# Sandwich layer (clustered attention, then a mixture of experts), one core: routing per group of tokens, rows sent to regions, three held chunks instead of two

## What is computed

```python
x = x + ln(attn(ln(x)))         # attn: qk = x@Wqk, v = x@Wv; per batch and head (16 heads of 16 channels)
                                #   softmax over channel-by-channel distances of qk, times v, then @ Wo
h = layernorm(x, g, b)          # rows of 256
logits = h @ Wr                 # 7 routed experts; top 2, gates = softmax of the two logits
pos = place of each (token, choice) in its expert's queue, first choices of ALL tokens before second ones
keep = pos < 732                # capacity of each expert
routed = sum over kept choices of gate * (silu(xe@W1[e]) * (xe@W3[e])) @ W2[e]
shared = (silu(h@W1s) * (h@W3s)) @ W2s      # every token, hidden width 1024
x = x + ln(routed + shared)
```

## Time and profile before

| | us |
|---|---|
| median of 3 runs | 1268.76 (1264.95 to 1269.63) |
| the profiled execution, own time | 1270.08 |
| its span, first to last instruction | 1268.3 |
| PE busy | 1128.9 (89%) |
| DVE busy | 724.9 (57%) |
| POOL busy | 391.4 (31%) |
| mean granted TensorE clock | 0.941 of full |

### The profile page before, as it was taken

How to read it: one execution, slowest core, us unless ns; L and a number is a source line. 1 busy time by engine, 2 the same in 40 slices (tenths; PEclk the granted TensorE clock), 3 DMA queues, 4 the chain that set the end, 5 groups by cost and what they waited for, 6 DMA issues and landing times.

```text
span 1268.3 us, 20395 instructions
## 1 busy us (share of the span) xinstructions
PE 1128.9 (89%) x6932; PEld 1033.2 (81%) x6932; DVE 724.9 (57%) x1541; ACT 519.3 (41%) x916; POOL 391.4 (31%) x321
## 2 busy tenths in 40 slices
PE   3557999999999999999998698999999999999760
PEld 2456888988888888888887597999999999998650
DVE  4445684464764564845667994445354454454885
ACT  2313343434434344343444212545455455453543
POOL 4523120131210230300312485144343434213554
PEclk9566999999999999999998898999999999999985
DMA  4206212044110044110353103244253242255773
GB/s 141 83 17 226 74 51 67 13 145 177 52 52 30 34 151 151 67 51 17 103 180 100 34 1 111 81 119 113 47 129 91 73 124 54 42 163 163 237 260 130
DMA packets 84004, 125.38 MB, mean 99 GB/s; under 512 B 8645, under 2 KB 68553, under 8 KB 83921
## 3 DMA queue, kind: packets, MB, share of 16 engines
q1 hardware_dynamic: 73728, 113.80, 27.0%
q0 software_dynamic: 10192, 10.52, 4.9%
HBM read 76.30 MB, written 47.98 MB: 98 GB/s over the span
## 4 chain that ended last, share of the span: by engine, by line
PE 72%; DVE 9%; issue 8%; POOL 6%; ACT 3%; DMA 2%; SPq 1%; POOLq 0%; ACTq 0%; DVEq 0%
PE bank L975 21%; PE bank L976 21%; PE bank L977 21%; PE bank L997 2%; PE bank L1077 2%; POOL sb_t_scale L772 2%; DVE sb_st L1206 1%; PE bank L1179 1%; PE bank L1069 1%; DVE sb_x L1477 1%; POOL sb_x L436 1%; ACT sb_ln_o L817 1%; PE bank L987 1%; DVE sb_act L1358 1%; PE bank L1015 1%
## 5 line engine op out<-in xcount | busy, mean ns | idle before, releaser
L1358 DVE TENSOR_TENSOR sb_act<-bank,sb_act 128x512 f32<-128x512 f32 (+2 forms) x240 | 148.7, 620 | 406.5 <-PE bank L977 365.8
L975 PE MATMUL bank<-sb_h_hi,sb_wup_lo 128*128 128x512 f32 (+2 forms) x960 | 354.8, 370 | 18.1 <-DVE sb_h_lo L1345 9.1
L976 PE MATMUL bank<-sb_h_lo,sb_wup_hi 128*128 128x512 f32 (+2 forms) x960 | 351.0, 366 | 0.0
L977 PE MATMUL bank<-sb_h_hi,sb_wup_hi 128*128 128x512 f32 (+2 forms) x960 | 349.6, 364 | 0.0
L899 ACT ACTIVATE sb_act<-bank 128x512 f32<-128x512 f32 (+2 forms) x240 | 130.1, 542 | 477.0 <-PE bank L977 434.2
L975 PE MATMUL bank<-sb_wdn_hi,sb_act_lo 128*128 128x256 f32 (+1 forms) x848 | 252.6, 298 | 24.4 <-DVE sb_act_lo L1351 22.4
L977 PE MATMUL bank<-sb_wdn_hi,sb_act_hi 128*128 128x256 f32 (+1 forms) x848 | 241.2, 284 | 0.0
L976 PE MATMUL bank<-sb_wdn_lo,sb_act_hi 128*128 128x256 f32 (+1 forms) x848 | 241.0, 284 | 0.0
L975 PEld LDWEIGHTS bank<-sb_h_hi,sb_wup_lo 128*128 128x128 f32 x960 | 183.9, 192 | 36.6 <-issue 11.9
L977 PEld LDWEIGHTS bank<-sb_h_hi,sb_wup_hi 128*128 128x128 f32 x960 | 182.9, 191 | 22.0
L976 PEld LDWEIGHTS bank<-sb_h_lo,sb_wup_hi 128*128 128x128 f32 x960 | 183.9, 192 | 16.3
(11 more groups left out here) (195 smaller groups left out, 1452.5 us busy)
## 6 DMA issues: line engine op xcount, KB each, us to landing
sb_xin<-in_L_ffn_W_dram SPq DMA_DIRECT2D x28, 512.0 KB
sb_xin<-in_L_attn_x_dram SPq DMA_DIRECT2D x16, 512.0 KB, 3.6
sb_x<-in_L_attn_x_dram SPq DMA_DIRECT2D x16, 512.0 KB, 5.1
x_scratch<-sb_x SPq DMA_DIRECT2D x16, 512.0 KB, 5.7
u_scratch<-sb_u SPq DMA_DIRECT2D x16, 512.0 KB, 3.2
hT_scratch<-sb_hr SPq DMA_DIRECT2D x16, 512.0 KB, 2.8
sb_hfull<-hT_scratch SPq DMA_DIRECT2D x16, 512.0 KB, 3.9
y_scratch<-sb_ysb SPq DMA_DIRECT2D x14, 512.0 KB, 2.8
```

Source lines behind the costliest of these rows:

```text
L975: t_.matmul(o, a_lo, b_hi, start=start, stop=False, skip_group_check=True)
L976: t_.matmul(o, a_hi, b_lo, start=False, stop=False, skip_group_check=True)
L977: return t_.matmul(o, a_hi, b_hi, start=False, stop=stop, skip_group_check=True)
L1358: v.tensor_tensor(act[:, m % 2, 0:c.w], bank[(4 if c.wide and m % 2 else 0) + 1][:, 0:c.w], act[:, m % 2, 0:c.w], ALU.mult).then_inc(act_o ...
```

## The change

What it does:

- `u_route` on DVE now finds both choices of the group's 4 tiles (13 small instructions where 1 was). New steps `u_count` (PE: 11 small bf16 matmuls) and `u_slot` (DVE: 9 small instructions) 2 places later give every token the row it is sent to: region = (choice, expert), 768 rows each, or a spare row.
- POOL sends the rows: per group `u_send0..3`, in all 8 indirect writes of 128 rows of 258 values (256 of `u`, the token's number, the difference of its two logits), at timetable places 57, 61, 84 and 88 (+0..3). The first send of a group waits until the one before has landed. 128 such writes in all. `u` has four buffers; its plain store is gone.
- The routing over all tokens (stage 3 above) is gone; what is left is `indices`: 5 small DVE instructions, at place 9 of the only chunk there.
- `HELD` = 3: one shared chunk in stage 3, three in stage 5. `IN_HELD` = 15, spread over 40 places (`LAST_AT`). The third held chunk's `hfull` is loaded behind the first y loads.
- In stage 3 the low halves of expert 0's weights are DVE's (6 pieces), not POOL's.
- In stage 1 SP clears the regions: 15 transfers, 11776 rows of 1032 bytes, at places 14 to 27. SP waits for all constants first.
- PE turns both halves of `u`, and for b > 0 of `xn`, through bank 7 only, with a wait on the copy of the first half. POOL computes e^(difference) per expert chunk, DVE the gates (4 small instructions) and the scatter indices (1 copy).

Cut to its core:

```diff
-    HELD = 2
+    HELD = 3
+    UW = D + 2
+    SENT = 2 * GT * 16
+    ROOM = ST * P
-        IN_HELD = (2 * FM * HELD - LAST0) // 2
+        IN_HELD = min((2 * FM * HELD - LAST0) // 2, NG - 1)
+        LAST_AT = [LAST0 + g * (2 * FM * HELD - LAST0) // IN_HELD for g in range(IN_HELD)]
+        TIMES = 2 * PLACES - LEAD
         for q in range(GB):
             for name, at in (("o_mix", 0), ("o_stats", 1), ("o_norm", 3), ("o_add", 4), ("u_stats", 6),
-                             ("u_norm", 9), ("u_turn0", 10), ("u_turn1", 11), ("u_route", 12)):
+                             ("u_norm", 9), ("u_turn0", 10), ("u_turn1", 11), ("u_route", 12), ("u_count", 14),
+                             ("u_slot", 14)):
                 timetable[38 + 4 * q + at].append((name, q))
+        for q, at in enumerate((57, 61, 84, 88)):
+            for t in range(GT):
+                timetable[at + t].append((f"u_send{t}", q))
...
+                if place in CLEAR_AT:
+                    sp.dma_start(sent_t[CLEAR_AT.index(place)], zrow[:, :].rearrange("p (a w) -> p a w", a=1
+                                 ).broadcast_to([P, ST, UW])).then_inc(none_in, 16)
...
+            def u_send(t):
+                def step(b, q):
+                    if t == 0:
+                        pool.wait_ge(r_slot, OPEN + b * GB + (q + 1))
+                        if isinstance(b, int) and b == 0 and q == 0:
+                            pool.wait_ge(none_in, (2 * E + 1) * 16)
+                        elif q > 0:
+                            pool.wait_ge(sent[q - 1], b * SENT + SENT)
+                        else:
+                            pool.wait_ge(sent[GB - 1], b * SENT)
+                        pool.sem_inc(pool_go, 1)
+                    for c in range(2):
+                        pool.indirect_dma_start(sent_d, bass.IndirectOffsetOnAxis(ap=sendto[:, q, t, c:c + 1], axis=0),
+                                                u[q][:, t, :], None).then_inc(sent[q], 16)
+                return step
...
-            for place in range(PLACES - LEAD, PLACES):
+            for place in range(PLACES - LEAD, TIMES):
                 attend(steps, place, B - 1)
-            for j in range(PIECES):
-                low_piece(1, j, 1, stage_later)
-            pool.wait_ge(r_slots, 1)
-            for n in range(NBLK):
...
                 def step(b, q):
                     if k == 0:
                         pe.wait_ge(u_ok, OPEN + b * GB + (q + 1))
-                        pe.wait_ge(lg_ok, OPEN + b * GB + q)
+                        pe.wait_ge(xtlo_ok, OPEN + b * (2 * GB) + 2 * GB)
+                    pe.wait_ge(hT_ok, OPEN + b * (2 * GB) + (2 * q + k))
                     for t in range(GT):
-                        ins = t_.transpose(bank[6 + k][:, t * P:(t + 1) * P], u[:, t, k * P:(k + 1) * P], ident[:, :])
+                        ins = t_.transpose(bank[7][:, t * P:(t + 1) * P], u[q][:, t, k * P:(k + 1) * P], ident[:, :])
...
+            def u_count(b, q):
+                pe.wait_ge(r_oh, b * GB + (q + 1))
+                t_.matmul(counts, earlier[:, :], oh[:, :, :, :].rearrange("p t c e -> p (t c e)"),
+                          start=True, stop=False, skip_group_check=True)
+                of = [oh[:, t, :, :].rearrange("p c e -> p (c e)") for t in range(GT)]
+                for t in range(1, GT):
+                    for s in range(t):
+                        t_.matmul(counts[:, t * 2 * E:(t + 1) * 2 * E], onesb[:, :], of[s],
+                                  start=False, stop=False, skip_group_check=True)
+                for t in range(GT):
+                    ins = t_.matmul(totals, onesb[:, :], of[t], start=False, stop=(t == GT - 1),
+                                    skip_group_check=True)
+                ins.then_inc(r_cnt, 1)
...
             def u_route(b, q):
...
+                for c in range(2):
+                    ch.link(v.tensor_reduce(best[:, c, :], lg[:, :, :], AX.X, ALU.max))
+                    ch.link(v.tensor_tensor(same[:, :, :], lg[:, :, :], over_e(best[:, c, :]), ALU.is_equal))
+                    ch.link(v.tensor_tensor(same[:, :, :], same[:, :, :], of_e, ALU.mult))
+                    ch.link(v.tensor_reduce(first[:, :], same[:, :, :], AX.X, ALU.max))
+                    ins = v.tensor_tensor(oh[:, :, c, :], same[:, :, :], over_e(first[:, :]), ALU.is_equal)
...
+            def u_slot(b, q):
+                dve.wait_ge(r_cnt, g + 1)
...
+                ch.step(v.tensor_copy(sendto[:, q, :, :], pos[:, :, :]))
+                ch.settle()
+                dve.sem_inc(r_slot, 1)
...
             def last_pass(place):
-                if place >= LAST0:
-                    g = (place - LAST0) // 2
-                    if place % 2 == 0:
-                        last_stats(g)
-                    else:
-                        if g > 0:
-                            last_add(v, dve, g - 1, DVE_TILES, t_ok)
-                        last_bias(g)
+                if place in LAST_AT:
+                    last_stats(LAST_AT.index(place))
+                elif place - 1 in LAST_AT:
+                    g = LAST_AT.index(place - 1)
+                    if g > 0:
+                        last_add(v, dve, g - 1, DVE_TILES, t_ok)
+                    last_bias(g)
```

More of the change, by code:

```diff
@@ L350, in held_chunks, with stored @@
         def held_chunks(body, between=lambda place: None):
-            body(expert_chunk(E - 1, 1, 1), held_chunk(0), held_chunk(1), between)
-            body(held_chunk(0), held_chunk(1), None, lambda place: between(2 * FM + place))
+            seq = [expert_chunk(E - 1, 1, 1)] + [held_chunk(h) for h in range(HELD)] + [None]
+            for h in range(HELD):
+                body(seq[h], seq[h + 1], seq[h + 2], lambda place: between(2 * FM * h + place))
+        def stored(s):
+            return sum((n + HELD) % 2 == s for n in range(FIRST))
         NCH = NG + 2 * E
@@ L565, in _ @@
                 sp.sem_inc(sp_go, 1)
-            for j in range(PIECES):
+            for j in range(3):
+                load_piece(1, j, [W1[0], W3[0]], W2[0], stage_later)
+            if HELD < GB - 1:
+                load_h(b, 1)
+            for place in range(PLACES - LEAD, TIMES):
+                attend(steps, place, b)
+            for j in range(3, PIECES):
                 load_piece(1, j, [W1[0], W3[0]], W2[0], stage_later)
@@ L597, in _ @@
                 sp.dma_start(last_y[k], last_view(y_d[0:T, :], k)).then_inc(t_y[k], 16)
+            for h in range(2, HELD):
+                load_held(h)
             for g in range(NG):
@@ L1195, in _ @@
             for m in (FM - 2, FM - 1):
-                down(held_chunk(1), m)
+                down(held_chunk(HELD - 1), m)
         @block.vector
@@ L1337, in _, with low_piece @@
                      "m_softmax": m_softmax, "m_low": m_low, "o_stats": o_stats, "o_norm": o_norm,
-                     "u_stats": u_stats, "u_norm": u_norm, "u_route": u_route}
-            def prep(c):
+                     "u_stats": u_stats, "u_norm": u_norm, "u_route": u_route,
+                     "u_slot": u_slot}
+            def low_piece(w, j, wset, stage):
+                hi, lo, src = piece(j, wset, stage)
+                dve.wait_ge(w_hi, w * PIECES + (j + 1))
+                v.tensor_tensor(lo, src, hi.bitcast(F32), ALU.subtract).then_inc(w_lo, 1)
+            def prep(c):
+                if c.expert is not None:
+                    par = 1 - c.wset
+                    dve.wait_ge(gathered[c.slot], c.landed)
+                    if not (isinstance(c.expert, int) and c.expert < 2):
+                        dve.wait_ge(added[c.slot], c.expert * (16 * HALF) - 16 * HALF)
+                    v.tensor_copy(scur[:, par, c.slot, :], rows[:, c.slot, 0:HALF, TOK]).then_inc(e_dst, 1)
                 dve.wait_ge(hhi_ok, c.n + 1)
@@ new lines, in route @@
+            def route(place):
+                if place % 2 and 5 <= place < 5 + 2 * PIECES:
+                    j = (place - 5) // 2
+                    if j == 4:
+                        dve.wait_ge(sent[0], B * SENT)
+                    low_piece(1, j, 1, stage_later)
+                if place == INDEX_AT:
+                    indices()
+            cs = [None] + last_chunks() + [None]
+            for j in range(1, len(cs) - 1):
+                body(cs[j - 1], cs[j], cs[j + 1], lambda place: beside_last(steps, route, 2 * FM * (j - 1) + place))
```

507 lines of the change are left out of this document (232 added, 275 removed).

## The result

The changed kernel takes 1346.56 us (median of 4 runs, 1344.79 to 1346.73) against 1267.53 before; the ratio is 1.0621, 95% interval 1.0597 to 1.0645. The forecast was 1261, with a range of 1240 to 1296: wrong in sign and in size. The profiled execution took 1346.66, 76.6 us more than that of before.

A forecast was written before the change was run, and what follows sets the result against it. PE was taken to bound the loop and experts, DVE the last batch and final stage. Middle -62, final stage +15, loop +33, attention +5, experts +1 gave -8 from 1270.1: 1262, median 1261 us, range 1240 to 1296.

The forecast's parts named there:

- The sends at places 28 to 43 fall in a gap of POOL and cost nothing: Loop: POOL's later sends add 0 us; without the gap they would cost x_part a wait.
- The top of a turn: Loop: PE 5.0 us late behind POOL's sends and x_rstd, plus 0.8 us for bank 7 alone.
- A: Whole kernel: the time as summed, 1261 us, own range 1246 to 1276; chance 0.45.
- The final stage: Final stage: one more chunk moves here, DVE stays the bound; +15 us.
- little lost where steps sit at odd places: Final stage: steps at odd places raise DVE's 98.5 us to 102 us.
- a whole chunk costs 15 and not 33: Final stage: a tail of 4 groups without PE becomes one of 1, so a chunk costs 15 us, not 33.
- Attention alone: Attention alone: +1 us for the residual behind the clearing, +4 us for DVE's added steps; +5 us.
- Rival D: Attention alone: the clearing holds up the residual by 8 to 25 us, total 1269 to 1286; chance 0.08.
- the middle: Last batch's chunk to the experts' first matmul: POOL's sends set its length; -62 us.
- the end of a turn: Loop: DVE's u_slot adds 2.9 us and u_route 2.5, so PE ends the turn 5.2 us later.
- Rival C: Loop and middle: a send costs 1.95 us like the scatter, turn above 195 us, total 1313; chance 0.17.
- Rival E: Loop: POOL and DVE block each other, u_norm above 3 us beside sends, total 1273; chance 0.12.

The follow-up runs named there:

- own_buffer: Changed kernel with the buffers of groups 0 and 3 exchanged, so m_sum waits for group 0's sends; 1294.96 us, ratio to before 1.021.
- even_places: Changed kernel with the final pass's 15 groups at every second place from 8 to 36; 1320.16 us, ratio to before 1.0411.
- changed_third: The changed kernel, unchanged, run again on one chip with even_again; 1347.46 us.
- even_again: The kernel of even_places, unchanged, run again on one chip with changed_third; 1338.08 us.
- the first four runs: own_buffer, clear_late, even_places and held_2, each one edit to the changed kernel, on one chip; 1294.96, 1318.35, 1320.16 and 1300.84 us.
- held_2: Changed kernel with two shared chunks of the last batch beside the final pass, not three; 1300.84 us, ratio to before 1.0256.
- clear_late: Changed kernel with the 15 clearing transfers at SP's places 27 to 40, behind the residual's first two loads; 1318.35 us, ratio to before 1.0409.
- the mended kernels: Changed kernel with buffers exchanged, sends spread, clearing behind the residual: three chunks held, final groups at even places, 1278.32 us; two held, 1261.10 us.

## Why the prediction was wrong

- **The step that failed first**: "The sends at places 28 to 43 fall in a gap of POOL and cost nothing". (They stand at 28 to 35.) POOL has the gap, but the changed kernel adds a wait for those very sends to `m_sum`, at a place ahead of them in DVE's program. I listed who waits for POOL's later powers and not who waits for the transfers. 11.9 us a turn, 36 in all, shown by own_buffer; without this wait the turn is 191 us where 189 to 190 was said.
- **The top of a turn**: 5.0 and 0.8 forecast. On a chip without late semaphores the rest of the turn agrees (even_places: turns of 202.0 and 202.5, less 11.9 for m_sum, less 178.1 and 178.6 before: 12.0, against 11). On the chips of the measurement it is 6 to 7 more a turn, 19 to 21 in all, which neither A nor a rival had. That it goes with the chip and not with the program was shown by changed_third and even_again, whose one program differs by 17.9. The mechanism assumed there (16 sends of POOL hold x_rstd, PE late at x_turn by 5.0) is at work on the chip of the first four runs, but small: in even_places x_rstd follows the last send at once, 0.7 to 2.2 us after DVE was ready for it. On the chips of the measurement it is not what held PE: x_rstd waited for DVE. The first two rows are even_places, the third is the changed kernel, whose last send ended at 371.7.

```profile
364.23 0.96 POOL L716 DMA_INDIRECT sent_scratch<-sb_rows,sb_sendto  x1 [0.30 <-issue]
365.21 1.05 POOL L683 TENSOR_TENSOR sb_rstd<-sb_veA,sb_mhalf 128x4 f32<-128x4 f32 x1
...
377.98 1.04 POOL L683 TENSOR_TENSOR sb_rstd<-sb_veA,sb_mhalf 128x4 f32<-128x4 f32 x1 [6.29 <-DVE sb_veA L1259]
```

- **The final stage**, 15 forecast, 30.9 measured. "15 x 4.7 + 20 x 1.22" compared DVE's sum with PE's sum and took the larger. The limit acts block by block: a block with a group takes DVE's 5.9 to 6.05, one without takes PE's 4.2: 15 x 6.05 + 5 x 4.2 = 112 instead of 98.5. The "little lost where steps sit at odd places" was 7.4 to 9.4 and not 3.5 us, since a group that crosses the border of two blocks slows both. That "a whole chunk costs 15 and not 33" made three held chunks look good; held_2 shows 31 (23 at even places) against 4.5 saved.
- **Attention alone**, 5 forecast, 12.6 measured up to u_turn of group 3. The transfer time of the clearing was right (33 us estimated; SP was rid of 13 of 15 in 30.1 us, and 298 GB/s were moved in them), the residual behind them was not: it landed 11.9 us after its issue, and the sum left some 4 for that. Rival D's sign, a residual behind 90, came true (91.66), but the sum it holds up was 6.3 us late and not 8 to 25. clear_late gave 8 us back at u_turn of group 3 on its chip.
- **Right**: the send, 1.3 us forecast from start to start, 0.96 and 0.30 measured; the middle, -62 and -62.4, bounded by POOL's sends; nearly the end of a turn, 5.2 (its two terms, 2.9 and 2.5, make 5.4), with 3.9 and 4.5 between u_turn of groups 1 and 2 (4.4 and 4.8 in own_buffer). Rival C had the side and nearly the turn (above 195) but not the cause: its condition, sends of 1.4 us or more, is not met. Rival E, u_norm slowed beside sends to over 3 us, is refuted: its four instructions took 1.38 to 1.42 us beside two sends, and 1.37 to 1.39 elsewhere in the loop.

The place of the excess over the forecast of 84.6 us: m_sum 36, the late semaphores 19 to 21, the final stage 16, attention alone 8, experts 2; the remaining 2 to 4 lie in the loop.

## What to carry to other kernels

When a buffer is emptied by a slow queue and shared with another stage, ask at which place of the other stage's program its wait stands and at which place of the queue's program the transfers are issued; a gap of the issuing engine is worth nothing if the wait comes ahead of it. Where work is woven into blocks, take the larger limit per block and then sum, and keep a group of steps inside one block. Work that waits for a resource that the change makes the bound (here POOL's sends in the middle) is the cheapest place for a chunk: moving the chunk away saved 4.5 us (8.2 in the mended kernels) and cost 31 (23 at even places).

## What was not expected of the hardware

- The same program differed by 18 us between two chips (1320.2 and 1338.1) on which the kernel before took the same time (1266.6 and 1267.5), and each was repeatable within 0.6%. The profiles differ in how late PE's semaphores come beside POOL's indirect transfers: 0.85 us or 4.4 us from a turn to its copy. Variants of such a kernel compare only on one chip.
- A wait of PE costs more than its length. Each stop of 9.3 to 9.6 us ahead of the product with Wqk was followed by 2 to 3 us of further delay up to m_dots; in own_buffer, without the stop, neither is there. The granted clock was 0.50 in the 4 us behind the stop and 0.95 over the turn, against 1.00 before.
- 774 KB of clearing with rows of 1032 bytes took SP 2.4 us per transfer (median) to get rid of, where a 512 KB load took 0.37 with the queue empty.
